# Reordering each engine's instruction list in a pipelined attention and spiking-network kernel on one core

## What is computed

```python
xn = layernorm(x)
h  = layernorm(xn) * ln_scale + ln_bias
c_q, c_kv = h @ w_down_q.T, h @ w_down_kv.T            # 64 each
q, k, v = rope(c_q @ w_up_q), rope(c_kv @ w_up_k), c_kv @ w_up_v   # 16 heads of 64
out = x + (softmax(q k.T / 8) @ v) @ w_out.T + xn
f = square(relu(xn @ W_fc.T)) @ W_proj.T               # 512 hidden
out += (number of spikes of a 5-step neuron fed with f) / 5
```

## Time and profile before

| | us |
|---|---|
| median of 3 runs | 1187.81 (1187.14 to 1190.89) |
| the profiled execution, its own time | 1185.65 |
| its span in the trace | 1183.8 |
| PE busy | 1001.8 (85%) |
| ACT busy | 923.8 (78%) |
| DVE busy | 900.7 (76%) |
| POOL busy | 895.0 (76%) |
| granted TensorE clock, mean | 0.99 |

### The profile page before, as it was taken

How to read it: one execution, slowest core, us unless ns; L and a number is a source line. 1 busy time by engine, 2 the same in 40 slices (tenths; PEclk the granted TensorE clock), 3 DMA queues, 4 the chain that set the end, 5 groups by cost and what they waited for, 6 DMA issues and landing times.

```text
span 1183.8 us, 25999 instructions
## 1 busy us (share of the span) xinstructions
PE 1001.8 (85%) x6880; PEld 734.1 (62%) x6880; DVE 900.7 (76%) x1223; ACT 923.8 (78%) x3008; POOL 895.0 (76%) x897
## 2 busy tenths in 40 slices
PE   3669888888888898888889888889888888988967
PEld 2546666666666666666666666666666666666644
DVE  3687878877778787787888777878778787877852
ACT  3678787888887888878787888888788888878751
POOL 3657977877887887787787788778778778778831
PEclk9899999999999999999999999999999999999989
DMA  5277667767776766776776677677677677767770
GB/s 165 90 199 210 173 189 204 180 190 197 194 191 187 202 181 189 212 178 190 199 184 187 191 203 186 191 196 186 188 206 186 187 194 188 191 185 199 202 173 24
DMA packets 93281, 217.96 MB, mean 184 GB/s; under 512 B 22464, under 2 KB 43200, under 8 KB 93120
## 3 DMA queue, kind: packets, MB, share of 16 engines
q1 hardware_dynamic: 92864, 216.52, 68.7%
q10 hardware_dynamic: 384, 1.05, 0.4%
HBM read 7.77 MB, written 4.19 MB: 10 GB/s over the span
## 4 chain that ended last, share of the span: by engine, by line
issue 27%; SPq 26%; POOL 21%; DVE 7%; PE 7%; DMA 6%; ACT 5%; POOLq 1%; ACTq 1%; DVEq 0%
SPq L255 25%; POOL partner L884 10%; POOL u_sb L928 6%; ACT prob L561 4%; DVE turned L740 4%; DMA x_sb<-in_x 3%; DMA resid<-early 3%; POOL qk L887 2%; PE ps_b L449 2%; POOL rstd L899 1%; DVE qk L724 1%; PE ps_u L343 1%; POOL early L910 1%; PE ps_qk L317 1%; PE ps_s L327 1%
## 5 line engine op out<-in xcount | busy, mean ns | idle before, releaser
L561 ACT ACTIVATE prob<-ps_s,neg_max 128x256 f32<-128x256 f32 x1024 | 474.3, 487 | 27.6 <-DVE neg_max L729 27.6
L884 POOL TENSOR_TENSOR partner<-partner,rope_sb 128x512 f32<-128x512 f32 x256 | 327.5, 1279 | 166.9 <-DMA partner<-raw 166.9
L740 DVE STREAM_TRANSPOSE turned<-prob 128x1024 f32<-128x1024 f32 x256 | 316.2, 1235 | 111.0 <-ACT prob L561 109.3
L887 POOL TENSOR_TENSOR qk<-qk,partner 128x512 f32<-128x512 f32 x256 | 325.8, 1273 | 20.1
L729 DVE TENSOR_REDUCE neg_max<-ps_s 128x4 f32<-128x1024 f32 x256 | 299.9, 1200 | 4.6 <-PE ps_s L327 4.6
L327 PE MATMUL ps_s<-qk 64*128 64x256 f32 x2048 | 267.7, 395 | 32.3 <-ACT prob L561 24.4
L573 ACT COPY raw<-ps_qk 128x512 f32<-128x512 f32 x256 | 150.2, 587 | 152.1 <-PE ps_qk L318 147.8
L327 PEld LDWEIGHTS ps_s<-qk 64*128 64x128 f32 x2048 | 188.2, 187 | 108.6 <-issue 75.6
L343 PE MATMUL ps_u<-gathered,ckv 128*64 128x256 f32 x2048 | 251.7, 388 | 0.0
L561 ACT ACTIVATION_READ_ACCUMULATOR prob<-ps_s,neg_max 128x1 f32 x1024 | 223.2, 218 | 0.0
L317 PE MATMUL ps_qk<-latent,wup_hi 128*128 128x256 f32 x512 | 166.8, 348 | 42.7 <-DVE qk L724 39.5
(11 more groups left out here) (67 smaller groups left out, 880.7 us busy)
## 6 DMA issues: line engine op xcount, KB each, us to landing
gathered<-turned SPq DMA_DIRECT2D x1016, 128.0 KB, 2.3
partner<-raw SPq DMA_DIRECT2D x256, 256.0 KB, 2.4
x_sb<-in_x SPq DMA_DIRECT2D x32, 128.0 KB, 2.1
resid<-early SPq DMA_DIRECT2D x32, 128.0 KB, 2.0
out<-out_sb SPq DMA_DIRECT2D x32, 128.0 KB, 2.0
turned<-in_wup SPq DMA_DIRECT2D x2, 512.0 KB, 5.8
gathered<-turned ACTq DMA_DIRECT2D x8, 128.0 KB, 4.9
rope_sb<-in_rope SPq DMA_DIRECT2D x1, 512.0 KB, 6.9
```

What stands on the lines that cost most here:

```text
L561: last = nc.scalar.activation(prob[:, s % 2, :, h, :, t, :].rearrange("p j k c -> p k j c"), ps_s[:, s % 2, h, t, :].rearrange("p (k j c) ...
L740: nc.vector.transpose(turned[:, par, :, s % GROUP, :], prob[:, s % 2, :, :, :, :, :].rearrange("p j h k t c -> p j (h k t c)"))\
L884: nc.gpsimd.tensor_tensor(other, other, sin_sb, ALU.mult).then_inc(sin_ready, 1)
L887: nc.gpsimd.tensor_tensor(qk[:, s % RING, :, :], qk[:, s % RING, :, :], other, ALU.add).then_inc(rope_done, 1)
```

## The change

No operation is added, removed or altered; each engine issues the same ones in another order. PE's `behind_first` and `behind_second` are gone, and each `step` function has its own list for q0, q1, q2 and q3. The new lists, with a and b for the two halves of a stage:

- SP: q0: exchange. q1: store(b-2), keep_residual(b), exchange, move. q2: exchange. q3: load_x(b+4), exchange, move.
- PE: q0: scores a, project a, scores b, latents, latents_by_token, project b, weigh. q1: broadcast 0, scores a, scores b, broadcast 1, project a, ffn_out both halves, broadcast 2, project b, weigh, broadcast 3. q2: project a, scores a, scores b, weigh, attention_out 0, project b, attention_out 1, ffn_in 0. q3: scores a, scores b, project a, ffn_in 1, attention_out 2 and 3, weigh, project b, transpose_sum, transpose_inputs, transpose_rden.
- ACT, DVE, POOL: as the diff has them. `copy_spread` 0 and 1 stand at the end of q0, 2 in q1, 3 at the head of q2; `inverse_std` and `split_sums` of POOL and `moments_of` and `invert_sums` of DVE are in q0.

In the diff below, indentation is cut and "..." stands for the lines that are taken out, all of which are in the functions printed above.

```diff
@@ -284,19 +284,31 @@
 g, b0, q = i * BODY + s, s // PAIRS, s % PAIRS // 2
 b = i * UNROLL + b0
 ahead, last = s + LEAD["project"] + 1, s + LEAD["scores"] + 1
...
+raws = not outside(g + LEAD["project"], STEPS)
+if q == 0:
+    if raws:
+        exchange(i * BODY + ahead, ahead)
+elif q == 1:
     if not outside(b - 2, B):
         store(b - 2, b0)
     if not outside(b, B):
         sp.wait_ge(res_ready, done(b))
         keep_residual(b0)
+    if raws:
+        exchange(i * BODY + ahead, ahead)
+    if last % GROUP == GROUP - 1 and not outside(i * BODY + last, STEPS):
+        move(i, last, (0, 1) if isinstance(g, int) and i * BODY + last == STEPS - 1 else (0, 1, 2, 3))
+elif q == 2:
+    if raws:
+        exchange(i * BODY + ahead, ahead)
+else:
+    if not outside(b + 2, B) and not outside(b + 4, B):
+        sp.wait_ge(res_ready, done(b + 2))
+        load_x(b + 4, b0)
+    if raws:
+        exchange(i * BODY + ahead, ahead)
+    if last % GROUP == GROUP - 1 and not outside(i * BODY + last, STEPS):
+        move(i, last, (0, 1) if isinstance(g, int) and i * BODY + last == STEPS - 1 else (0, 1, 2, 3))
 run(sp, prologue, step)
 for b in (B - 2, B - 1):
@@ -470,60 +482,6 @@
                                     start=True, stop=True)
 last.then_inc(setup_pe, 1)
...
 def prologue():
 start_counters(pe, "pe")
 pe.wait_ge(w_input, INPUT_LOADED)
@@ -533,17 +491,96 @@
 def step(i, s):
 g, b0, q = i * BODY + s, s // PAIRS, s % PAIRS // 2
 b = i * UNROLL + b0
...
+near, far = LEAD["scores"], LEAD["project"]
+scored, projected = not outside(g + near, STEPS), not outside(g + far, STEPS)
+spread = not outside(b - 1, LAST)
+if q == 0:
+    if is_last(b - 1):
+        last_attention_out(b - 1, 3, 1 - b0)
+        transpose_sum(b - 1)
+    if scored:
+        scores(g + near, s + near)
+    if projected:
+        project(g + far, s + far, i)
+    if scored:
+        scores(g + near + 1, s + near + 1)
+    if not outside(b + 1, B) and not outside(b + 2, B):
+        latents(b + 2, b0)
+    if not outside(b + 1, B):
+        latents_by_token(b + 1, 1 - b0)
+    if projected:
+        project(g + far + 1, s + far + 1, i)
+    if not outside(g, STEPS):
+        weigh_latents(g, s, i)
+elif q == 1:
+    if spread:
+        broadcast_rden(b - 1, 0)
+    if scored:
+        scores(g + near, s + near)
+        scores(g + near + 1, s + near + 1)
+    if spread:
+        broadcast_rden(b - 1, 1)
+    if projected:
+        project(g + far, s + far, i)
+    if not outside(b, B):
+        ffn_out(b, 0)
+        ffn_out(b, 1)
+    if spread:
+        broadcast_rden(b - 1, 2)
+    if projected:
+        project(g + far + 1, s + far + 1, i)
+    if not outside(g, STEPS):
+        weigh_latents(g, s, i)
+    if spread:
+        broadcast_rden(b - 1, 3)
+    if is_last(b):
+        transpose_last_rden(b)
+elif q == 2:
+    if projected:
+        project(g + far, s + far, i)
+    if scored:
+        scores(g + near, s + near)
+        scores(g + near + 1, s + near + 1)
+    if not outside(g, STEPS):
+        weigh_latents(g, s, i)
+    if spread:
+        attention_out(b - 1, 0, 1 - b0)
+    if projected:
+        project(g + far + 1, s + far + 1, i)
+    if spread:
+        attention_out(b - 1, 1, 1 - b0)
+    if not outside(b + 1, B):
+        ffn_in(b + 1, 0, 1 - b0)
+    if is_last(b):
+        broadcast_last_rden(b)
+else:
+    if is_last(b):
+        last_attention_out(b, 0, b0)
+        last_attention_out(b, 1, b0)
+    if isinstance(b, int) and b == -2:
+        value_by_output()
+    if scored:
+        scores(g + near, s + near)
+        scores(g + near + 1, s + near + 1)
+    if projected:
+        project(g + far, s + far, i)
+    if not outside(b + 1, B):
+        ffn_in(b + 1, 1, 1 - b0)
+    if spread:
+        attention_out(b - 1, 2, 1 - b0)
+        attention_out(b - 1, 3, 1 - b0)
+    if not outside(g, STEPS):
+        weigh_latents(g, s, i)
+    if projected:
+        project(g + far + 1, s + far + 1, i)
+    if not outside(b - 1, B):
+        transpose_sum(b - 1)
+    if not outside(b + 3, B):
+        transpose_inputs(b + 3, 1 - b0)
+    if not outside(b, LAST):
+        transpose_rden(b)
+    if is_last(b):
+        last_attention_out(b, 2, b0)
 run(pe, prologue, step)
@@ -665,53 +702,87 @@
 def step(i, s):
 g, b0, q = i * BODY + s, s // PAIRS, s % PAIRS // 2
 b = i * UNROLL + b0
...
+near, far = LEAD["scores"], LEAD["project"]
+raws, exps = not outside(g + far, STEPS), not outside(g + near, STEPS)
 spread = not outside(b - 1, LAST)
 if q == 0:
+    if isinstance(b, int) and b == -1:
+        copy_value_by_output()
+    if raws:
+        copy_projected(g + far, s + far, i)
     if spread:
         copy_rden(b - 1)
+    if exps:
+        exponentials(g + near, s + near, i)
+    if raws:
+        copy_projected(g + far + 1, s + far + 1, i)
+    if exps:
+        exponentials(g + near + 1, s + near + 1, i)
+    if not outside(b + 1, B) and not outside(b + 2, B):
+        lead_latents(b + 2, b0)
+    if not outside(b + 1, B):
+        copy_latents(b + 1, 1 - b0)
+    if spread:
+        copy_spread(b - 1, 0)
+    if not outside(g, STEPS):
+        copy_u(g, s, i)
     if not outside(b, B):
         square(b, 1)
...
+    if spread:
+        copy_spread(b - 1, 1)
+elif q == 1:
+    if raws:
+        copy_projected(g + far, s + far, i)
+    if exps:
+        exponentials(g + near, s + near, i)
+    if raws:
+        copy_projected(g + far + 1, s + far + 1, i)
+    if spread:
+        copy_spread(b - 1, 2)
+    if exps:
+        exponentials(g + near + 1, s + near + 1, i)
+    if not outside(g, STEPS):
+        copy_u(g, s, i)
+    if not outside(b + 3, B):
+        normalise(b + 3, 1 - b0, 1)
+    if is_last(b):
+        copy_last_rden(b)
+elif q == 2:
+    if spread:
+        copy_spread(b - 1, 3)
+    if raws:
+        copy_projected(g + far, s + far, i)
+    if exps:
+        exponentials(g + near, s + near, i)
+    if not outside(g, STEPS):
+        copy_u(g, s, i)
+    if raws:
+        copy_projected(g + far + 1, s + far + 1, i)
+    if exps:
+        exponentials(g + near + 1, s + near + 1, i)
+    if not outside(b + 1, B):
+        relu(b + 1, 0)
 else:
     if not outside(b + 3, B):
...
+        normalise(b + 3, 1 - b0, 0)
+    if raws:
+        copy_projected(g + far, s + far, i)
+    if exps:
+        exponentials(g + near, s + near, i)
+        exponentials(g + near + 1, s + near + 1, i)
+    if not outside(b + 1, B):
+        relu(b + 1, 1)
+    if raws:
+        copy_projected(g + far + 1, s + far + 1, i)
+    if not outside(g, STEPS):
+        copy_u(g, s, i)
     if not outside(b + 3, B):
         copy_inputs(b + 3, 1 - b0)
     if not outside(b + 1, B):
         square(b + 1, 0)
...
+    if is_last(b + 1):
+        move_last(2)
+        move_last(3)
 run(act, prologue, step)
@@ -825,52 +896,86 @@
 def step(i, s):
 g, b0, q = i * BODY + s, s // PAIRS, s % PAIRS // 2
 b = i * UNROLL + b0
...
+near, far = LEAD["scores"], LEAD["project"]
+rotates, turns = not outside(g + far, STEPS), not outside(g + near, STEPS)
+if q == 0:
+    if is_last(b - 1):
+        normalise_last(b - 1, 3, 1 - b0)
+    if not outside(b - 2, B):
+        finish(b - 2, b0, i - 1)
     if not outside(b, LAST):
         invert_sums(b, b0)
...
+    if turns:
+        row_max(g + near, s + near)
+    if rotates:
+        rotate(g + far, s + far)
+    if turns:
+        row_max(g + near + 1, s + near + 1)
+    if not outside(b + 1, B) and not outside(b + 3, B):
+        moments_of(b + 3, 1 - b0, i + 1 + b0)
+    if rotates:
+        rotate(g + far + 1, s + far + 1)
+    if turns:
+        turn(g + near, s + near, i)
+        turn(g + near + 1, s + near + 1, i)
+    if not outside(b + 1, B) and not outside(b + 2, B):
+        split_latents(b + 2, b0)
+    if is_last(b):
         invert_sums(b, b0)
...
+    if is_last(b - 1):
+        add_spikes(b - 1, 1 - b0)
+        finish(b - 1, 1 - b0, i - 1)
+elif q == 1:
+    if turns:
+        row_max(g + near, s + near)
+    if rotates:
+        rotate(g + far, s + far)
+    if turns:
+        row_max(g + near + 1, s + near + 1)
+    if not outside(b, B):
+        integrate(b, b0, 0)
+        integrate(b, b0, 1)
+    if rotates:
+        rotate(g + far + 1, s + far + 1)
+    if not outside(b, B):
+        integrate(b, b0, 2)
+    if turns:
+        turn(g + near, s + near, i)
+        turn(g + near + 1, s + near + 1, i)
+elif q == 2:
+    if not outside(b, B):
+        integrate(b, b0, 3)
+    if turns:
+        row_max(g + near, s + near)
+    if rotates:
+        rotate(g + far, s + far)
+    if not outside(b, B):
+        integrate(b, b0, 4)
+    if turns:
+        row_max(g + near + 1, s + near + 1)
+        turn(g + near, s + near, i)
+    if rotates:
+        rotate(g + far + 1, s + far + 1)
+    if turns:
+        turn(g + near + 1, s + near + 1, i)
+    if is_last(b):
         normalise_last(b, 0, b0)
         normalise_last(b, 1, b0)
...
+else:
+    if turns:
+        row_max(g + near, s + near)
```

(61 more changed lines are left out.)

136 lines of the change are left out of this document (removed).

## The result

The changed kernel takes 1049.89 us, median of 4 runs (1048.6 to 1050.79), against 1187.47 for the kernel before in the same comparison: a ratio of 0.8838, 95% interval 0.8814 to 0.8861. The profiled execution took 1048.6, 1.8 more than its span of 1046.8.

The account below looks back on a forecast made before the run. A loop of waits, not a full engine, bound the kernel at 34.9 us a batch. Forecast: 71.9 + 30 x 31.2 + 60 = 1067.9 span, 1069.8 with 1.85 outside, 1072 after the 2.2 median offset; range 1051 to 1126.

Parts of the forecast that it names:

- PE becomes the bound: Middle of the kernel: PE's own work of 30.8 us per batch sets the limit, with loads 31 to 31.5 us apart.
- rival A: New stalls at interleaved ps_qk and ps_b, such as broadcast 1's wait for a copy: period 33, 1126 us; chance 0.28.
- rival B: The q1 loop, 28.8 us plus POOL's q0 waits, makes it slower: period 36 at 7.2 us of waits, 1216; chance 0.06.
- rival C: No change: an unseen loop has today's length and reordering leaves it, 1187 to 1189 us; chance 0.03.
- part 1: SP: load of x goes ahead of the q3 exchange and move, saving 0.58 us between move and exchange.
- part 2: SP: store and keep_residual go ahead of the q1 exchange and move, costing nothing; cover gone, 1 us of move delay.
- part 3: Last two normalisations go to POOL's q1; second copy leaves the way to the q3 turn; new q3 loop 27.3 us.
- part 5: PE: projections between the scores, broadcasts in q1; all five lists walked, 0.4 us added for stalls, period 31.2.
- The walk: All five new lists followed for one batch with trace durations; closes to 0.2 us except POOL, PE bound at 30.8 us.
- the fill: Start up to the first weighing: taken as it is, 71.92 us, give or take 3.
- the end: From the first weighing of batch 30 on: 60 us instead of 65.1, 5 us less, bounds 0 and 8.
- Rival D: PE's matmuls could run closer together, so ACT's 28.9 us is the next bound: 1012 us; chance 0.03.

Follow-up runs that it names:

- experiment 2: The kernel before with SP's new list alone: 1168.33 us, ratio 0.9842.
- experiment 12: The kernel before with SP's new list and POOL's normalisation 3 moved ahead of inverse_std and the rope in q2: 1116.53 us, ratio 0.9417.
- experiment 5: The changed kernel with the first score matmul of each pair issued twice: 1141.51 us, ratio 0.961.
- experiment 6: The changed kernel without the low part of the up-projection weights, 16 matmuls fewer per batch: 1027.87 us, ratio 0.8646.
- experiment 1: The changed kernel with SP's old list put back, the load of x in q0 behind the q3 move: 1388.36 us, ratio 1.1701.
- experiment 9: The changed kernel with value_by_output, the 32 set-up matmuls, put back behind the projections of its step: 1050.57 us, ratio 0.885.
- experiment 3: The changed kernel with POOL's old list put back: 1289.44 us, ratio 1.0864.
- experiment 4: The changed kernel with PE's old list put back: 1469.86 us, ratio 1.2395.

## Why the prediction was right or wrong

**Right: the bound of before.** The loop from the q3 move over the exchange, POOL's q1 and q2, normalisation 3, chunk 3, the projection, exponentials and turn. Experiments 2 and 12 took two terms out of it, with 18 and 52 us where 18 and 38 to 51 were expected.

**Right: PE becomes the bound.** Period 30.84 against PE's own 30.8; busy 99.6% in the middle; experiment 5. Rivals A, B and C did not come. Of the places that rival A names, the copy ahead of a broadcast costs PE 1.1 us in 400 even in experiment 6, with less PE work; the small margin at scores b of q3 is one of the two at which that kernel waits.

**Right: parts 1 and 2.** Loads and stores ahead of the moves cost nothing, and SP's new list alone gives the 0.6 us a batch. Part 1 has moments_of far behind the load, and did not price what that distance is worth: without it the period is 42.6 (experiment 1). The early load and the new place of moments_of belong together.

**Wrong in a detail: part 3.** It takes the second copy of raw off the way to the q3 move. The move stands behind the exchange, which needs that copy, and the trace has it start behind the exchange (556.60). While PE is the bound this costs nothing that the runs show.

**Wrong: part 5, the 0.4 us a batch added for stalls.** The walk gave 30.8; I did not trust its small margins and took 31.2. PE's idle time in the middle is 1.55 us in 13 batches, 0.12 a batch: the term was next to nothing. From first weighing to first weighing the trace has (990.47 - 67.27) / 30 = 30.77, so the allowance and rounding cost 12.9 us of the 21.1 between the span predicted (1067.9) and measured (1046.8). The margins of 0.05 to 1 us did not turn into stalls. I take the reason to be that each batch runs like the last, so that a margin, once positive, stays so; no run tests that by itself. That the walk closed to 0.1 us is in part luck: it is 0.2 to 0.45 us early from the second scores of q0 to the scores of q1, and its own two stalls, 0.25 and 0.4 us, which the trace hardly has, make up for it. The 30.8 of PE's work from the earlier trace rows does not hang on that.

**Wrong in size: the fill**, "taken as it is": 67.27 in place of 71.92, 4.6 us. I had not walked the first seven steps; experiment 9 gives 1.5 to 4.3 of it to value_by_output.

**Wrong in size: the end.** 56.3 in place of 60. The second weighing of the last batch came 36.5 us after the first weighing of batch 30 (990.47 to 1026.98), where I had 37.3 (1118.66 to 1156): nearly right. The larger part, 2.9 us, is behind it, where I left the old 22.7 us (1161.09 to 1183.8) and the trace has 19.8: the new q2 weighs ahead of the output chunks, so the third weighing, at 1029.71, follows the second by 2.7 us. PE's timeline, with the first weighing of batch 0, that of batch 30, and the second and third of the last batch:

```profile
67.27 1.95 PE L355 MATMUL ps_u<-gathered,ckv 128*64 128x256 f32 x16
...
990.47 1.95 PE L355 MATMUL ps_u<-gathered,ckv 128*64 128x256 f32 x16
...
1026.98 1.95 PE L355 MATMUL ps_u<-gathered,ckv 128*64 128x256 f32 x16
...
1029.71 1.95 PE L355 MATMUL ps_u<-gathered,ckv 128*64 128x256 f32 x16
```

These three are what put the time 1.1 us below the low end. Its terms were a period of 30.8, a fill of 71.9 less 3, an end of 57, 4 outside the span, and the rest of its 5 off, 2, for rival D. They make 1052; the 1051 in the prediction is a slip. Every term came in under its bound: the fill by 1.6, the period by 0.8 in 30 batches, the end by 0.7, and what lies outside the span, 3.1 for 4, by 0.9. The 2 us for rival D took up half of that.

**Rival D and the rule.** By the rule of the Trainium skill ("Perfetto Trace Analysis", section "Identifying the Most-Contended Engine"), weight loads at 62% meant room in PE. In the middle of the changed kernel the loads are busy 294.83 of 400 us, 74%, PE's matmuls 99.6%, and experiment 5 shows the time to follow PE's work at 0.93. In this kernel the matmul busy time, 30.7 us a batch of a period of 30.8, was the better measure of the room that reordering has.

**Where the loop arithmetic failed** was in the experiments: periods of 37.9, 33.7 and 34.8 computed, 42.6, 39.1 and 44.4 measured. Each time I followed one loop or one stall by name, and at full clock. A walk of all five lists, as in part 5, should have met the waits of ACT and PE that closed longer loops; it was not done for these kernels, and it would have lacked the time lost to the clock.

## What to carry to other kernels

When engines of similar load work through fixed lists, walk all lists together for one period, with durations from the trace, and bound the period from below by the fullest engine. Do not judge one engine's list by itself: three of the new lists were taken back one at a time, and each time the kernel became 9% to 24% slower than the old one. Look for the operation that stands between a wait and the next move on the closed loop; moving one POOL operation of 1.27 us ahead of the inverse_std and the rope of its step gave 4.4%.

## What was not expected of the hardware

**A stall is paid for twice.** The busy view of three stretches of experiment 1, around PE's wait for split_latents (537.9 to 547.35):

```profile
530.00:540.00 10.00, 7.86 (x58) 5.54 (x58) 3.02 (x4) 8.25 (x27) 4.61 (x4) 0.99 0.91 225
540.00:550.00 10.00, 2.65 (x8) 2.37 (x9) 6.44 (x12) 1.32 (x5) 5.94 (x10) 0.50 0.29 92
550.00:560.00 10.00, 10.00 (x66) 7.10 (x65) 7.91 (x12) 7.26 (x26) 9.76 (x9) 0.83 0.25 78
```

The granted clock was 0.50 (1.2 GHz) in the stretch from 540, in which PE stood until 547.35 and came back, and the eight ffn_out matmuls took 3.62 us where they take 1.89 at full clock. Mean clocks are 0.872, 0.906 and 0.885 in experiments 1, 3 and 4, and 0.99 in both main kernels. PE's busy time rose as the clock fell (1000.8 to 1067.2, 1072.4 and 1131.0), which is a part of what the loop sums missed. The low clock lengthens the very loop that makes the stall; that this keeps the stall alive is argued and was not tried by itself. The kernel before had PE idle for 1.64 us at a time and kept 1.00.

**A score matmul done again costs more than its share.** The four score matmuls of a pair, eight records, take 0.96 us on PE in their normal order, in which the two heads, on the lower and the upper 64 rows, alternate: 0.24 us each. The repeated one, on the lower 64 rows ahead of another there that writes the same place, added 0.39 us, 1.6 times its share. That the heads overlap when they alternate would explain the rest, and so would a cost of writing the same place twice; neither was tried by itself.
